# A four-layer gated Flamingo kernel on one core: routing steps, weight splits and transposes in another order, returned rows in two loads

## What is computed

```
x = x + tanh(g_xattn[0]) * attention0(layernorm(x), ctx)   # 16 heads of 64, w_q, w_kv, w_out, second layer norm inside
x = x + tanh(g_ffn[0])   * moe0(layernorm(x))              # 8 experts 128->256->128, relu, gates of the best 2
x = x + tanh(g_xattn[1]) * attention1(layernorm(x), ctx)   # 1 head of 128, Wq, Wk, Wv
x = x + tanh(g_ffn[1])   * moe1(layernorm(x))              # shared expert + 8 experts 128->512->128, silu, best 2

moe0:  probs = softmax(x @ gate_w + gate_b); the two largest are the weights
       out = sum_e weight[e] * (relu(x @ w1[e] + b1[e]) @ w2[e] + b2[e])
moe1:  gates = softmax(relu(x @ Wr1 + br1) @ Wr2 + br2); tg = softmax(top2(gates) / 2)
       out = silu(x @ Ws1 + bs1) @ Ws2 + bs2
             + sum_e w[e] * (silu(x @ We1[e] + be1[e]) @ We2[e] + be2[e])
```

## Time and profile before

| | us |
|---|---|
| median of 3 runs | 306.22 |
| lowest and highest | 304.85, 306.44 |
| the profiled execution | 306.4 |
| its span in the profile | 304.7 |

### The profile page before, as it was taken

How to read it: one execution, slowest core, us unless ns; L and a number is a source line. 1 busy time by engine, 2 the same in 40 slices (tenths; PEclk the granted TensorE clock), 3 DMA queues, 4 the chain that set the end, 5 groups by cost and what they waited for, 6 DMA issues and landing times.

```text
span 304.7 us, 6266 instructions
## 1 busy us (share of the span) xinstructions
PE 279.6 (92%) x2157; PEld 240.0 (79%) x2157; DVE 192.5 (63%) x607; ACT 167.0 (55%) x354; POOL 96.0 (32%) x144
## 2 busy tenths in 40 slices
PE   1999988789989989899999899999899999999995
PEld 0577865668878767788888699779689889999985
DVE  2798952688899997346767757655867722432106
ACT  2493346698886766423334564586716722556460
POOL 1167000666883443103006441010101540155510
PEclk9999999799999999999999999999999999999999
DMA  7799950000000000072000000000000145931122
GB/s 183 247 318 273 205 90 2 1 2 4 20 12 2 1 2 0 2 227 88 0 2 0 0 2 1 1 2 0 2 1 2 47 154 156 296 104 39 45 83 73
DMA packets 20526, 20.49 MB, mean 67 GB/s; under 512 B 2097, under 2 KB 15049, under 8 KB 20496
## 3 DMA queue, kind: packets, MB, share of 16 engines
q1 hardware_dynamic: 19088, 18.09, 22.1%
q0 software_dynamic: 1120, 1.88, 2.2%
q10 hardware_dynamic: 288, 0.13, 0.2%
HBM read 15.86 MB, written 4.24 MB: 66 GB/s over the span
## 4 chain that ended last, share of the span: by engine, by line
PE 65%; DVE 19%; POOL 5%; issue 4%; ACT 3%; DMA 2%; SPq 0%; DVEq 0%; ACTq 0%; POOLq 0%
PE bank L1251 10%; PE bank L1430 9%; PE bank L1224 7%; PE bank L1225 6%; PE bank L1226 6%; PE bank L1411 4%; PE bank L1418 4%; DVE xhat_sb L907 4%; PE bank L1209 4%; POOL p_sb L642 3%; DVE sum_sb L844 3%; PE bank L1169 2%; DMA ctx_tok_sb<-in_ctx 2%; PE bank L1180 2%; DVE negmax_sb L833 2%
## 5 line engine op out<-in xcount | busy, mean ns | idle before, releaser
L785 ACT ACTIVATE hT_sb<-bank,cols_sb 128x512 f32<-128x512 f32 x72 | 48.6, 689 | 52.9 <-PE bank L1226 52.4
L642 POOL TENSOR_TENSOR p_sb<-p_sb,recip_sb 128x480 f32<-128x480 f32 x32 | 31.6, 988 | 52.2 <-DVE recip_sb L847 52.2
L1146 DVE SCALAR_TENSOR_TENSOR x_sb<-bank,wts_sb,x_sb 128x128 f32<-128x128 f32 x96 | 27.0, 344 | 26.2 <-PE bank L1430 17.2
L1251 PEld LDWEIGHTS bank<-we_sb,hT_sb 128*128 128x128 f32 x320 | 37.1, 192 | 1.2 <-issue 0.5
L1251 PE MATMUL bank<-we_sb,hT_sb 128*128 128x128 f32 x320 | 38.0, 276 | 0.0
L694 POOL TENSOR_TENSOR rstd_sb<-veps_sb,minus_half_sb 128x4 f32<-128x4 f32 (+1 forms) x11 | 11.0, 998 | 66.8 <-DVE veps_sb L899 66.5
L1430 PE MATMUL bank<-w_sb,hT_sb 128*128 128x128 f32 x256 | 31.5, 276 | 0.0
L1430 PEld LDWEIGHTS bank<-w_sb,hT_sb 128*128 128x128 f32 x256 | 30.4, 192 | 1.2 <-issue 0.4
L1180 PE MATMUL bank<-ident_sb,p_sb 128*120 128x128 f32 x128 | 19.8, 280 | 7.7 <-POOL p_sb L642 7.4
L795 ACT ACTIVATE p_sb<-bank,bias_t_sb 128x128 f32<-128x128 f32 x60 | 17.0, 369 | 16.7 <-PE bank L1411 16.7
L1180 PEld LDWEIGHTS bank<-ident_sb,p_sb 128*120 128x120 f32 x128 | 13.6, 138 | 11.6 <-issue 10.1
(11 more groups left out here) (217 smaller groups left out, 610.1 us busy)
## 6 DMA issues: line engine op xcount, KB each, us to landing
xs_hbm<-col_rows_sb SPq DMA_DIRECT2D x1, 2145.0 KB, 17.5
we_sb<-in_L_ffn_We SPq DMA_DIRECT2D x1, 2048.0 KB, 8.8
w_sb<-in_L_ffn_We SPq DMA_DIRECT2D x8, 256.0 KB, 4.1
w_after_sb<-in_L_ffn_We SPq DMA_DIRECT2D x7, 256.0 KB, 3.4
w_kv_sb<-in_L_xattn_w_kv SPq DMA_DIRECT2D x2, 512.0 KB, 6.8
w_sb<-in_L_ffn_w SPq DMA_DIRECT2D x1, 1024.0 KB, 9.7
w_kv_sb<-xs_hbm SPq DMA_DIRECT2D x15, 65.0 KB, 3.1
x_sb<-in_x SPq DMA_DIRECT2D x1, 512.0 KB, 7.2
```

The costliest lines, as they stand in the source:

```text
L642: nc.gpsimd.tensor_tensor(p0[j % 4], p0[j % 4], recip0[:, j % 2, :].unsqueeze(2) .broadcast_to([128, HG, SK]), ALU.mult).then_inc(probs_re ...
L785: nc.scalar.activation(hT[:, u % 2, c, :], ps(item)[:, :], ACT.Relu if n == 1 else ACT.Silu, bias=cols[:, col:col + 1]).then_inc(read(item ...
L1146: last = nc.vector.scalar_tensor_tensor(out=x[:, b, :], in0=ps(key)[:, C * i:C * (i + 1)], scalar=w, in1=x[:, b, :], op0=ALU.mult, op1=ALU ...
L1251: last = nc.tensor.matmul(ps(key)[:, C * i:C * (i + 1)], hT[:, unit_at[(n, p, e)] % 2, c, 128 * i:128 * (i + 1)], we2[:, e, c, :], start=( ...
```

## The change

It has four parts, all in the order of things or in how they are grouped; no arithmetic is added or left out.

1. **Routing of moe0, half 0, during attention.** "logits" moves ahead of attention step 30 (it stood behind it), "top" behind step 32 (it stood behind 31), "hot" next to "weights", behind step 33.
2. **The nine splits of moe1's first weights.** Six now stand between the routing steps of moe0's second half, ahead of "consts"; two follow near attention1's scores and transposes, the ninth three expert units later. Before, they stood one after each of nine steps, the first right behind "consts".
3. **"wT" of moe1, half 0**, moves from ahead of "o1" to behind the first two "up" items of the next expert and the "down" sums behind them.
4. **The end.** The returned rows come in two loads of 512 rows with one semaphore between them. "comb" moves ahead of the shared expert's sums and waits for both loads. The rows of half 1 are released for storing by the shared expert's sums. "down2" takes a bank from the first six.

```diff
--- before.py
+++ after.py
@@ -159,8 +159,8 @@
 
     early = first_done - 5
     ahead = {early: ("stats", 1, (0, HB // 2)), early + 1: ("xhat", 1, (0, HB // 2))}
-    spaced = dict(zip((0, 1, 4, 7, 8, 9, 10, 12), [("stats", 1, (HB // 2, HB)), ("xhat", 1, (HB // 2, HB)),
-                                                   ("xT", 1, 0), *route_items(1, 0)[:-1]]))
+    spaced = {0: [("stats", 1, (HB // 2, HB))], 1: [("xhat", 1, (HB // 2, HB))], 4: [("xT", 1, 0)],
+              6: [("logits", 1, 0)], 9: [("top", 1, 0)], 10: [("hot", 1, 0), ("weights", 1, 0)], 12: [("wT", 1, 0)]}
     tail = expert_units(0)[:3]
     for i in range(len(late_queries), STEPS + LY):
         schedule.append(("attend", i))
@@ -169,7 +169,7 @@
         if i in ahead:
             schedule.append(ahead[i])
         if i - first_done in spaced:
-            schedule.append(spaced[i - first_done])
+            schedule.extend(spaced[i - first_done])
 
         if i in (STEPS, STEPS + 2, STEPS + 4):
             add_units([tail.pop(0)], [])
@@ -185,18 +185,19 @@
                 [("xbias", 3, 0), ("logits", 3, 0), ("lexp", 3, 0)]]
     splits = [("split", "we1", i) for i in range(E + 1)]
     rest = add_units(expert_units(0)[n_tail:], [[("stats", 1, 1), ("b2", 1, 0)]] + one_by_one(
-        [("xhat", 1, 1), ("k1", 0), ("xT", 1, 1), ("logits", 1, 1), ("top", 1, 1), ("v1", 0),
-         ("hot", 1, 1), ("weights", 1, 1), ("k1", 1), ("v1", 1), ("wT", 1, 1), ("b2", 1, 1)]))
-    chain = [[]] + attend1[0] + into_ff1
+        [("xhat", 1, 1), ("k1", 0), ("xT", 1, 1)]) + [[item, split] for item, split in zip(
+            [("logits", 1, 1), ("top", 1, 1), ("v1", 0), ("hot", 1, 1), ("weights", 1, 1), ("k1", 1)], splits)]
+        + one_by_one([("v1", 1), ("wT", 1, 1), ("b2", 1, 1)]))
+    chain = [[("consts",)]] + attend1[0] + into_ff1
     chain = [(rest[k] if k < len(rest) else []) + items for k, items in enumerate(chain)]
-    chain = [splits[k:k + 1] + items for k, items in enumerate(chain)]
-    chain[0] = [("consts",)] + chain[0]
+    for k, split in zip((6, 8, 13), splits[6:]):
+        chain[k] = chain[k] + [split]
     rest = add_units(expert_units(1), chain)
     scatters = [("scatter", i) for i in range(HB)]
     rest = [[("stats", 2, 1)], sum(rest, []), [("xhat", 2, 1)], [("xT", 2, 1)], [("q1", 1)],
             [("s1", 1), ("s1exp", 1)], [("top", 3, 0), ("tau", 0)], [("hot", 3, 0), ("weights", 3, 0)], [("pT1", 1)],
-            [("wT", 3, 0), ("o1", 1), ("stats", 3, 1)],
-            [], [("xhat", 3, 1), ("b2", 3, 0)], [("xT", 3, 1)], [("r1", 1)],
+            [("o1", 1), ("stats", 3, 1)],
+            [("wT", 3, 0)], [("xhat", 3, 1), ("b2", 3, 0)], [("xT", 3, 1)], [("r1", 1)],
             [("logits", 3, 1), ("lexp", 3, 1), ("xbias", 3, 1)], [("top", 3, 1), ("hot", 3, 1)], [],
             [("rank",), *scatters],
             [("tiles",)], [("pages",)], [("tau", 1)], [("weights", 3, 1)],
@@ -206,7 +207,8 @@
         schedule.extend(items)
     tile_items()
     add_second_units(behind_tiles, [], None, [])
-    schedule.insert(-1, ("comb",))
+    summed = schedule.index(("down", *units[-2]))
+    schedule.insert(summed, ("comb",))
 
 
     def by_scalar(item):
@@ -242,7 +244,8 @@
             plan(item, 6 + downs % 2)
             downs += 1
         elif item[0] == "part" and (item[4] == 0 or item[1:] == (*units[-1], HB // 2)):
-            plan(part_key(item), 6 + downs % 2)
+            key = part_key(item)
+            plan(key, turn % 6 if key[0] == "down2" else 6 + downs % 2)
             downs += 1
         elif item[0] == "attend":
             i = step = item[1]
@@ -484,7 +487,7 @@
         w1_landed = [sem(f"w1_landed{j}") for j in range(TILES)]
         xs_landed = [sem(f"xs_landed{j}") for j in range(TILES)]
         scattered = sem("scattered")
-        gathered = [sem(f"gathered{i}") for i in range(HB)]
+        gathered = sem("gathered")
         tables_ready = sem("tables_ready")
         sel_ready = sem("sel_ready")
         tile_e_ready = sem("tile_e_ready")
@@ -581,10 +584,10 @@
                 load_w1(range(TG * (g + 1), min(TG * (g + 2), TILES)))
 
             sp.wait_ge(returned, 16 * TILES)
-            for i in range(HB):
-                for k in range(2):
-                    at = HALF * k + 1 + 128 * i
-                    sp.dma_start(y_of[:, k, i, :], ys_hbm[at:at + 128, :]).then_inc(gathered[i], 16)
+            for k in range(2):
+                at = HALF * k + 1
+                sp.dma_start(y_of[:, k], ys_hbm[at:at + HALF, :].rearrange("(i p) c -> p i c", p=128)) \
+                    .then_inc(gathered, 16)
 
             for i, b in enumerate([*range(HB, B), *range(0, HB, 2)]):
                 sp.wait_ge(x_ready, i + 1 if b >= HB else HB + b + 1)
@@ -1073,16 +1076,16 @@
                 elif kind == "dnt":
                     copy_out(item, x_rows[:, item[1], :], ps(item)[:, 0:C])
                 elif kind == "comb":
+                    dve.wait_ge(gathered, 16 * 2)
                     for i in range(HB):
                         b = HB + i
-                        dve.wait_ge(gathered[i], 16 * 2)
                         for k in range(2):
                             last = nc.vector.scalar_tensor_tensor(out=x[:, b, :], in0=y_of[:, k, i, :],
                                                                   scalar=comb_w[:, i, k:k + 1], in1=x[:, b, :],
                                                                   op0=ALU.mult, op1=ALU.add)
                             if k == 0:
                                 link(last)
-                        last.then_inc(x_ready, 1)
+                    link(last)
                 elif kind == "wT":
                     p = item[2]
                     copy_out(item, wtsT[:, HALF * p:HALF * (p + 1)], ps(item)[0:E, :])
@@ -1145,9 +1148,9 @@
                         w = wts[:, b, e:e + 1] if e < E else tanhs[:, 3:4]
                         last = nc.vector.scalar_tensor_tensor(out=x[:, b, :], in0=ps(key)[:, C * i:C * (i + 1)],
                                                               scalar=w, in1=x[:, b, :], op0=ALU.mult, op1=ALU.add)
-                        if item[1:] == units[-1]:
+                        if item[1:] in units[-2:]:
                             last.then_inc(x_ready, 1)
-                    if item[1:] != units[-1]:
+                    if item[1:] not in units[-2:]:
                         last.then_inc(read(item), 1)
                         wait_read(dve, item)
 
```

## The result

| | before | after |
|---|---|---|
| median us | 306.03 (17 runs) | 303.88 (17 runs) |
| lowest and highest | 304.85, 306.44 | 302.32, 305.48 |
| the profiled execution, its span | 306.4, 304.7 | 304.03, 302.3 |

The ratio after to before is 0.9935, with a 95% interval of 0.9921 to 0.9949: 2.0 us faster, between 1.6 and 2.4. The forecast was 304.6 us, a gain of 1.7.

A forecast was written before the change was run, and what follows sets the result against it. TensorE, busy 279.6 of 304.7 us, was taken as the bound. Terms -1.9 - 1.1 + 1.9 - 0.6 = -1.7 us took the profiled 306.4 to 304.7; 0.2 above the median, so forecast 304.6, range 302.6 to 306.2.

The forecast's parts named there:

- Part 1: Moe0 routing at the end of attention 0: gain 0.8 + 1.5 - 0.4 = 1.9 us, bounds 2.4 and 0.5.
- the 1.44 us: TensorE's third wait at the end of attention 0, for GpSimd's product; forecast to go.
- But the output product then waits for ScalarE's copy: End of attention 0: the output product begins behind ScalarE's copy, so TensorE idles 0.4 us again.
- attention loses in its chain: Rival: maximum, exponential and product of attention steps 30 and 31 come later; gain there 0.5 us, total 306.0; chance 0.17.
- L952 is not held up: Rival: VectorE's third small routing instruction is not held by GpSimd's product; gain there 2.4 us, total 304.1; chance 0.08.
- Part 2: Splits made earlier: "xhat" at 166.27 no longer slowed by GpSimd, gain 1.1 us; bound 0.5.
- The wait of 1.07 us: TensorE's wait at 169.39 for "xhat", slowed beside two GpSimd splits; forecast to go.
- Part 3: Moe1's "o1" still waits for VectorE's copy, "b2" idles TensorE 1.5 us: loss 1.9 us, bounds 0.4 and 2.2.
- that it does what it is shaped for: Rival for moving "wT": 1.15 us won or nothing lost; total 302.7, down to 301.6; chance 0.12.
- Part 4: The end: additions done before 297.6, so VectorE waits for TensorE's last matmul; gain 0.6 us.
- The estimate of 2.6 us for a load of 256 KB: Returned rows at the end: 2.0 us plus bytes by 436 GB/s, landing at 295.6 from the second issue.

The follow-up runs named there:

- part 1 alone: The kernel before with only the moved routing of moe0, half 0, during attention: 303.55 us, ratio 0.9906.
- the part alone: The kernel before with only "wT" of moe1, half 0, moved behind two "up" items: 308.45 us, ratio 1.0070.

## Why the prediction came out

The number was 0.7 us too high, and the range held the time. Of the 0.7, 0.45 is gain that was not forecast (2.15 between the medians against 1.7), 0.2 comes from before, whose median over 17 runs is 306.03 and not 306.22, and 0.1 from the sum: 306.22 - 1.7 is 304.5, not 304.6. By the stretches the gain is 2.7 to 3.0, so that the number is as near as it is has some luck in it. Step by step:

- **Part 1, mechanism right, one term wrong.** L955 with 0.78 us, the maximum at 115.01 (forecast 1.2 us late; it comes 1.22 behind the reciprocal and came 0.09 behind it before, so 1.13 late), the transposes at 118.33 with a smaller wait, and the 1.44 us gone: all as worked out. The step that failed is "But the output product then waits for ScalarE's copy ... TensorE idles 0.4 us again". The product of 122.23 began before the copy of 121.92 ended at 122.51. It belongs to batch 6, `attend(34)`, where the code has it read the copies made after steps 25 and 27; those of batch 7 come four items later. I had taken the copy next to it in time for the one it needs. Without that term part 1 is 2.3, and 2.40 was measured in after, 2.39 in part 1 alone. The rival "attention loses in its chain" is refuted by the same rows; "L952 is not held up" is refuted by the 0.78 us, though it would have given nearly the measured time.
- **Part 2, right and 0.16 us too small.** The wait of 1.07 us is gone, 1.26 were won. An idle entry counts from a modelled end, which overlaps the next start, so that it leaves out 0.16 us of the distance from start to start here (169.39 behind 167.92, against 166.10 behind 165.86 in after: 1.23 us more).
- **Part 3, right in each step.** "o1" waited for the copy, the sums came between, "b2" waited 1.41 us (forecast 1.5), and the stretch lost 1.8 (forecast 1.9). The rival, that it does what it is shaped for, is out: the part alone is 2.1 us slower.
- **Part 4, right, though not through the loads.** Landed by 294.6 where issues started at 290.84, 3.8 us behind, which in the frame of before is 296.3, as 296 was forecast; additions done before the sums; 0.7 us won against 0.6. But the argument leaned on the two loads being quicker than the eight, and the run with eight loads has the same time: it tested only whether all rows are there early, and the first pair already is 2.3 us behind the issue. The estimate of 2.6 us for a load of 256 KB does not fit either: the page's fit (the Trainium skill, page "DMA: Bandwidth & Descriptors", section "Anatomy of one DMA") is for DMAs issued from GpSimd, and these, issued from SP, landed 2.9 and 3.3 us behind their issues.

Of the table's five differences all but part 1's lie within 0.2 us of the forecast; that one is 0.8 off in after, 0.3 of it ahead of the changed part, and 0.5 in part 1 alone.

## What to carry to other kernels

When a wait is to be removed by moving work, look at the second instruction that the engine will then meet: if it needs the same neighbour, one place further down the same queue, the wait only changes its name, and the work that was moved is late later on. Move the producer instead (here VectorE's copy ahead of the weights), which by the stretch around it gave 3.1 us more than the move of the consumer, and 1.3 more than no move. And take a dependency from the code (which batch, which buffer number), never from what stands nearby in time.
